# Fp4 feed-forward of a one-core Trainium2 program: normalisation and rounding exponent moved to ScalarE, rounding in three VectorE operations, scales double-buffered

## The reference, cut to what matters

```
xb = x.reshape(..., n // 16, 16)
scale = jnp.maximum(jnp.max(jnp.abs(xb), -1, keepdims=True) / 6.0, 1e-12)
xn = xb / scale
idx = jnp.searchsorted(_MID, jnp.abs(xn))       # grid 0, 0.5, 1, 1.5, 2, 3, 4, 6
q = _GRID[idx] * jnp.sign(xn) * scale
...
def fp4_linear(x, w):                           # gate, up and down
    return einsum('bsk,nk->bsn', fp4_quant_dequant(x), fp4_quant_dequant(w))
```

## Time and profile before

| what | value |
|---|---|
| device time, median of 3 runs | 3646.06 us (3645.56 to 3650.42) |
| the profiled execution: its time, as the span from first to last instruction | 3752.3 us |
| mean granted TensorE clock in it | 0.915 |
| busy over the span: PE / DVE / ACT / POOL | 84% / 67% / 53% / 32% |
| first pass of the stage: first operation to start of its last `add` | 18.82 to 182.15 us |
| second pass: the same | 899.2 to 1059.46 us |

### The profile page before, as it was taken

How to read it: one execution, slowest core, us unless ns; L and a number is a source line. 1 busy time by engine, 2 the same in 40 slices (tenths; PEclk the granted TensorE clock), 3 DMA queues, 4 the chain that set the end, 5 groups by cost and what they waited for, 6 DMA issues and landing times. The chain is left out here.

```text
span 3752.3 us, 61710 instructions
## 1 busy us (share of the span) xinstructions
PE 3149.9 (84%) x20415; PEld 1980.8 (53%) x20415; DVE 2516.1 (67%) x6929; ACT 1992.9 (53%) x2981; POOL 1210.8 (32%) x1282
## 2 busy tenths in 40 slices
PE   4669999786659967999999599687778885998899
PEld 2533333344448842222222488566666674887687
DVE  8888997675974468999995744543585345666565
ACT  1238988663214446999999144322332234664564
POOL 3454550112456631101010566366434651001000
PEclk8879999997859988999999699799898897999899
DMA  1043430000021132000000411401201113000100
GB/s 55 1 130 124 131 126 13 1 1 23 1 115 42 43 103 61 27 20 28 20 20 2 168 42 43 140 29 44 75 24 61 43 40 113 1 1 1 65 9 12
DMA packets 87167, 187.18 MB, mean 50 GB/s; under 512 B 23168, under 2 KB 41408, under 8 KB 83792
## 3 DMA queue, kind: packets, MB, share of 16 engines
q1 hardware_dynamic: 60048, 117.66, 9.3%
q0 software_dynamic: 26816, 65.58, 5.7%
HBM read 121.23 MB, written 61.34 MB: 49 GB/s over the span
## 5 line engine op out<-in xcount | busy, mean ns | idle before, releaser
L2486 ACT ACTIVATE core_pr<-core_two 128x1024 f32<-128x1024 f32 (+3 forms) x896 | 787.6, 935 | 49.3 <-PE core_two L2453 45.5
L2522 DVE TENSOR_REDUCE core_mx<-core_one 128x1 f32<-128x512 f32 x778 | 491.8, 685 | 20.9 <-PE core_one L2405 13.6
L2465 PE MATMUL core_ps_o<-core_pr,core_vals 128*32 128x512 f32 (+3 forms) x3584 | 434.5, 560 | 1.8 <-ACT core_oT L2497 1.5
L2405 PE MATMUL core_one<-arena,queries 64*128 64x512 bf16 (+3 forms) x1472 | 375.5, 363 | 29.8 <-PEq L62 19.6
L2453 PE MATMUL core_two<-queries,arena 64*128 64x512 bf16 (+3 forms) x1792 | 341.5, 360 | 9.4 <-ACT core_pr L2486 6.8
L2405 PEld LDWEIGHTS core_one<-arena,queries 64*128 64x128 bf16 x1472 | 113.3, 94 | 297.7 <-DVE core_mx L2522 132.4
L2339 POOL COPY core_vals<-arena 128x288 f32<-128x288 f32 x32 | 14.7, 459 | 692.1 <-PE core_ps_o L2465 692.1
L2516 DVE CUSTOM_DVE_ANT_0 core_junk<-core_one,core_over 128x512 bf16<-128x512 f32 (+4 forms) x334 | 201.9, 644 | 26.2 <-PE core_one L2405 21.4
L2453 PEld LDWEIGHTS core_two<-queries,arena 64*128 64x128 bf16 x1792 | 94.3, 94 | 201.7 <-ACT core_pr L2486 145.7
L2492 ACT ACTIVATE core_over<-core_two 128x1024 f32<-128x1024 f32 (+4 forms) x167 | 159.9, 958 | 58.4 <-PE core_two L2428 45.3
L424 POOL DMA_INDIRECT expert_out<-arena,moe_second_dest_index x142 | 139.9, 985 | 149.9 <-ACT arena L600 129.9
(11 more groups left out here) (614 smaller groups left out, 8184.0 us busy)
## 6 DMA issues: line engine op xcount, KB each, us to landing
arena<-expert_out SPq DMA_DIRECT2D x64, 256.0 KB, 3.8
expert_rows<-arena SPq DMA_DIRECT2D x13, 512.0 KB, 12.5
core_w_raw<-in_m_up POOLq DMA_DIRECT2D x25, 256.0 KB, 3.4
m_hi<-core_w_hi POOLq DMA_DIRECT2D x25, 256.0 KB, 2.4
m_lo<-core_w_lo POOLq DMA_DIRECT2D x25, 256.0 KB, 3.0
q_parts<-qkv_parts SPq DMA_DIRECT2D x16, 384.0 KB, 2.6
k_parts<-qkv_parts SPq DMA_DIRECT2D x16, 384.0 KB, 3.4
queries<-q_parts SPq DMA_DIRECT2D x64, 96.0 KB
```

The costliest lines, as they stand in the source:

```text
L2405: pe.matmul(one[bank[e]][:, 0:width], q_sb[rows, hq, pair, qt * P:(qt + 1) * P], k_sb[rows, hq, pair, kc * CW:kc * CW + width], start=True ...
L2465: mm = pe.matmul(ps_o[h * 32:(h + 1) * 32, off:CW], vals[:, hq % 2, j, h, :], pr[:, (n * N2 + k) % KEPT, h // 2, h % 2, off:CW], start=(j ...
L2486: a.activation(pr[:, step % KEPT, i, :, off:CW], two[spot[e] % 2][:, :, off:CW], ACT.Exp, scale=HD ** -0.5).then_inc(s_wide, 1)
L2522: v.tensor_reduce(at, scores, AX.X, ALU.max).then_inc(s_read, 1)
```

## The change

In `ffn0_stage`:

- `normalise` moves from VectorE to ScalarE, as scale and shift of an activation. GpSimd's `power` gains two small operations for the shift (minus mean times reciprocal deviation) and a wait for `normalise` of two chunks before.
- The rounding exponent is made on ScalarE by a new method `grid`: the square of the divided value, then a linear map. `round` on VectorE waits for it and has three operations in place of four (exponent mask and half bit in one, add, subtract).
- `scale` and `inverse` have two buffers each, so that new scales wait for `back` of two chunks before, not of the last one.
- The orders are rewritten. VectorE: all four `hidden(c+1)` and `x_scales(c+4)` come before `add(c-1)`, `fh.round(c)` and `h_scales(c+1)`. GpSimd: `fh.divide(c)` first and `h_back(c)` last in a turn. TensorE: `finish(c-1)` in place of `finish(c)`, ahead of `turn(c+3)` and the `up` of chunk c+2. ScalarE: two `silu`, `normalise(c+4)`, the four copies of `finish(c-1)`, `fh.grid(c)`, `copy(c+3)`, two `silu`, `x_grid(c+4)`.

The diff, cut to its core:

```diff
--- before.py
+++ after.py
@@ -1396,6 +1396,11 @@
 FP4_MAGIC = 1.5 * 2.0 ** 22
 BELOW = 1.0 - 2.0 ** -24
 EXPONENT = 0x7F800000
+HALF_BIT = 0x00400000
+
+
+GRID_SLOPE = 2.0 ** 22 / 6.0
+GRID_START = 8.0 * 2.0 ** 22 / 6.0
 
 
 class Fp4:
@@ -1406,75 +1411,69 @@
 
 
 
-    VEC_OPS = 7
-
-    def __init__(self, st, g, name, blocks):
-        self.g, self.nb = g, blocks
+    SCALES, STEPS = 3, 3
+
+    def __init__(self, st, g, name, blocks, binade):
+        self.g, self.nb, self.binade = g, blocks, binade
         self.amax = st.sb(f"{name}_amax", [P, blocks])
-        self.scale = st.sb(f"{name}_scale", [P, blocks])
-        self.inverse = st.sb(f"{name}_inverse", [P, blocks])
+        self.scale = st.sb(f"{name}_scale", [P, 2, blocks])
+        self.inverse = st.sb(f"{name}_inverse", [P, 2, blocks])
         self.v = st.sb(f"{name}_v", [P, blocks * BLOCK])
         self.magic = st.sb(f"{name}_magic", [P, blocks * BLOCK])
 
...
+        self.s_scales, self.s_square, self.s_grid, self.s_steps, self.s_pool, self.s_out = (
+            st.sem(f"{name}_{n}") for n in ("scales", "square", "grid", "steps", "pool", "out"))
+
+    def cut(self, ap):
+        return ap.rearrange("p (b k) -> p b k", k=BLOCK)
+
+    def largest(self, v, src, r):
+        v.tensor_reduce(self.amax[:], src, AX.X, ALU.max, apply_absolute_value=True).then_inc(self.s_scales, 1)
+
+    def inverted(self, v, r):
+        at = r * self.SCALES
+        if r >= 2:
+            v.wait_ge(self.s_out, r - 1)
+        v.wait_ge(self.s_scales, at + 1)
+        v.tensor_scalar(self.scale[:, r % 2], self.amax[:], 1.0 / 6.0, 1e-12, ALU.mult, ALU.max).then_inc(self.s_scales, 1)
+        v.wait_ge(self.s_scales, at + 2)
+        v.reciprocal(self.inverse[:, r % 2], self.scale[:, r % 2]).then_inc(self.s_scales, 1)
+
+    def divide(self, p, src, r):
+        p.wait_ge(self.s_scales, (r + 1) * self.SCALES)
+        if r:
+            p.wait_ge(self.s_out, r)
+        p.tensor_tensor(self.cut(self.v[:]), src, self.inverse[:, r % 2].unsqueeze(2).to_broadcast([P, self.nb, BLOCK]),
+                        ALU.mult).then_inc(self.s_pool, 1)
+
+    def grid(self, a, r):
+
+        a.wait_ge(self.s_pool, r + 1)
+        a.activation(self.magic[:], self.v[:], ACT.Square).then_inc(self.s_square, 1)
+        a.wait_ge(self.s_square, r + 1)
+        a.activation(self.magic[:], self.magic[:], ACT.Identity, bias=self.binade[:], scale=GRID_SLOPE).then_inc(self.s_grid, 1)
+
+    def round(self, v, r):
+        x, b, at = self.v[:], self.magic[:], r * self.STEPS
+        v.wait_ge(self.s_grid, r + 1)
+        v.tensor_scalar(b.bitcast(U32), b.bitcast(U32), EXPONENT, HALF_BIT, ALU.bitwise_and, ALU.bitwise_or).then_inc(self.s_steps, 1)
+        v.wait_ge(self.s_steps, at + 1)
+        v.scalar_tensor_tensor(x, x, BELOW, b, ALU.mult, ALU.add).then_inc(self.s_steps, 1)
+        v.wait_ge(self.s_steps, at + 2)
+        v.tensor_tensor(x, x, b, ALU.subtract).then_inc(self.s_steps, 1)
+
+    def back(self, p, dst, r):
+        p.wait_ge(self.s_steps, (r + 1) * self.STEPS)
+        q, scale, nb = self.cut(self.v[:]), self.scale[:, r % 2], self.nb
+        wide = scale.unsqueeze(2).to_broadcast([P, nb, BLOCK])
...
     def wait_done(self, eng, r):
-        eng.wait_ge(self.s_out, r + 2)
+        eng.wait_ge(self.s_out, r + 1)
 
...
@@ -1582,8 +1581,10 @@
     st = Stage(nc, name, prefetch)
     f = Front(st, g)
     head = Head(st, g, ahead) if ahead else None
-    fx = Fp4(st, g, "zq", CW // BLOCK)
-    fh = Fp4(st, g, "hq", CT * FFN0 // BLOCK)
+    binade = st.sb("binade", [P, 1])
+    fx = Fp4(st, g, "zq", CW // BLOCK, binade)
+    fh = Fp4(st, g, "hq", CT * FFN0 // BLOCK, binade)
+    minus, shift = st.sb("minus", [P, 2, CT]), st.sb("shift", [P, 2, CT])
     xq = st.sb("xq", [P, 2, CT, P])
     s = st.sb("silu", [P, 2, FFN0])
     h = st.sb("h", [P, 2, CT, FFN0])
...
@@ -1608,37 +1609,21 @@
     with st.block() as block:
         @block.vector
         def _(v):
-            fx.on(v)
-            fh.on(v)
             v.sem_inc(s_h, 2)
             v.sem_inc(s_sum, 1)
-            v.memset(hq[:], 0.0).then_inc(s_zero, 1)
+            v.memset(binade[:], GRID_START).then_inc(s_binade, 1)
 
             def statistics(c):
                 if c <= last:
+                    if c >= 2:
+                        v.wait_ge(s_shift, c - 1)
                     f.statistics(v, c, c % 2)
 
-            def normalise(c):
-                if c > last:
-                    return
-                if c == 0 and f.head:
-                    v.sem_inc(f.s_xn, 1)
-                    return
-                v.wait_ge(f.s_rstd, c + 1)
-                if c >= 2:
-                    v.wait_ge(fx.s_pool, c - 1)
-                for k in range(CT):
-                    end = v.tensor_scalar(f.xn[:, c % 2, k, :], flat(tile_of(g.x, c * CT + k)), f.mv[:, c % 2, k, 0:1],
-                                          f.rstd[:, c % 2, k:k + 1], ALU.subtract, ALU.mult)
-                end.then_inc(f.s_xn, 1)
-
             def x_scales(c):
-                if c > last:
-                    return
-                v.wait_ge(f.s_xn, c + 1)
-                fx.largest(v, blocks(f.tiles(c)), c)
-                fx.scaled(v, c)
-                fx.inverted(v)
+                if c <= last:
+                    v.wait_ge(f.s_xn, c + 1)
+                    fx.largest(v, blocks(f.tiles(c)), c)
+                    fx.inverted(v, c)
 
             def x_round(c):
                 if c <= last:
@@ -1650,17 +1635,11 @@
                 v.wait_ge(s_silu, c * CT + t + 1)
                 v.tensor_tensor(h[:, c % 2, t, :], s[:, t % 2, :], ps_u[t % 2][:, 0:FFN0], ALU.mult).then_inc(s_h, 1)
 
...
+            def h_scales(c):
+                if c <= last:
+                    v.wait_ge(s_h, c * CT + CT + 2)
+                    fh.largest(v, blocks(h[:, c % 2]), c)
+                    fh.inverted(v, c)
 
             def add(c):
                 v.wait_ge(s_down, c + 1)
@@ -1669,40 +1648,34 @@
 
             statistics(0)
             statistics(1)
-            normalise(0)
             x_scales(0)
             statistics(2)
+            v.memset(hq[:], 0.0).then_inc(s_zero, 1)
             x_round(0)
-            normalise(1)
             x_scales(1)
+            statistics(3)
+            x_round(1)
             hidden(0, 0)
             hidden(0, 1)
-            statistics(3)
-            x_round(1)
-            normalise(2)
             x_scales(2)
             hidden(0, 2)
             hidden(0, 3)
-            h_largest(0)
+            h_scales(0)
             statistics(4)
             x_round(2)
-            normalise(3)
             x_scales(3)
-            h_inverses(0)
             for c in range(CHUNKS):
                 hidden(c + 1, 0)
                 hidden(c + 1, 1)
                 statistics(c + 5)
                 x_round(c + 3)
-                normalise(c + 4)
-                fh.round(v, c)
+                hidden(c + 1, 2)
+                hidden(c + 1, 3)
+                x_scales(c + 4)
                 if c:
                     add(c - 1)
-                hidden(c + 1, 2)
-                hidden(c + 1, 3)
-                h_largest(c + 1)
-                x_scales(c + 4)
-                h_inverses(c + 1)
+                fh.round(v, c)
+                h_scales(c + 1)
...
@@ -1712,8 +1685,22 @@
         @block.gpsimd
         def _(p):
             def power(c):
-                if c <= last:
-                    f.power(p, c, c % 2)
+                u = c % 2
+                if c > last:
+                    return
+                if c == 0 and f.head:
+                    p.sem_inc(f.s_ve, 1)
+                    p.sem_inc(s_minus, 1)
+                    p.sem_inc(f.s_rstd, 1)
+                    p.sem_inc(s_shift, 1)
+                    return
+                if c >= 2:
+                    p.wait_ge(f.s_xn, c - 1)
+                f.power(p, c, u)
+                p.tensor_scalar(minus[:, u, :], f.mv[:, u, :, 0], -1.0, None, ALU.mult).then_inc(s_minus, 1)
+                p.wait_ge(f.s_rstd, c + 1)
+                p.wait_ge(s_minus, c + 1)
+                p.tensor_tensor(shift[:, u, :], minus[:, u, :], f.rstd[:, u, :], ALU.mult).then_inc(s_shift, 1)
 
             def x_divide(c):
                 if c <= last:
@@ -1737,16 +1724,18 @@
             power(3)
             x_back(1)
             x_divide(2)
+            p.wait_ge(s_zero, 1)
+            fh.divide(p, blocks(h[:, 0]), 0)
             power(4)
             x_back(2)
             x_divide(3)
-            p.wait_ge(s_zero, 1)
             for c in range(CHUNKS):
-                fh.divide(p, blocks(h[:, c % 2]), c)
+                if c:
+                    fh.divide(p, blocks(h[:, c % 2]), c)
+                power(c + 5)
+                x_back(c + 3)
+                x_divide(c + 4)
                 h_back(c)
-                x_back(c + 3)
-                power(c + 5)
-                x_divide(c + 4)
...
@@ -1801,15 +1790,33 @@
```

(50 more changed lines are left out.)

60 lines of the change are left out of this document (4 added, 56 removed).

## The result

The changed kernel takes 3718.6 us (median of 4 runs, 3714.5 to 3729.3) where the kernel before takes 3647.8 beside it: ratio 1.0203, 95% interval 1.0187 to 1.0219, or 70.8 us more. I had predicted 3714 us (3676 to 3743), 90% for slower. The profiled execution took 3715.8 us.

The account below looks back on a forecast made before the run. A ring of waits across engines was to bound the kernel: three intervals of 21.57 us, three of 19.83 and one of 16.63 make 140.8 against 103.1; less 3 at the start, 69.4 us slower in both passes, 3714 us (3676 to 3743).

Parts of the forecast that it names:

- a ring: Waits from h rounding through scales, `hidden`, `up`, copies and grid to the next rounding: 21.57 us with `normalise`, 19.83 without.
- the hold: VectorE's small operation in h's scales is held until GpSimd's `h_back` ends, making the scales term 3.50 us instead of 2.62.
- the first rival: VectorE still bounds, with turns 2.77 us shorter while x lasts and 0.93 later: 3612 us, chance 7%.
- to TensorE: First `hidden` of chunk c+2 on VectorE, with a gap before it and the step to TensorE: 0.66 us.
- two `up`: Two `up` on TensorE behind its wait for `hidden`: 4.13 us, against 2.36 at full clock.
- to the first copy with `normalise`: From the two `up` to ScalarE's first copy: 2.3 us with `normalise` between, 0.56 without.
- copies: ScalarE's four copies of `finish` with TensorE's turns between them: 3.82 us.
- grid: ScalarE's square and map on h, 1.35 and 1.44 us, with gaps and the step to VectorE: 2.96 us.
- The last interval: Seventh interval between h roundings, with no `up` left: rounding, `h_back`, turns and copies at low clock, grid, 16.63 us.
- the rival of the low clock lasting into the copies: TensorE's turns and copies take 6.73 us instead of 4.38 in each of six intervals: 3742 us, chance 8%.
- The start: Before the first h rounding, VectorE loses work: gain between 0 and 8.8 us a pass, taken as 3.
- The table rival: Square and SiLU on ScalarE share no table, so the ring holds one more 1.28 us load: 3736 us, chance 6%.

Follow-up runs that it names:

- e1: Operations of the kernel before (`normalise` and four-step rounding on VectorE, single scales) in the changed kernel's order: 3726.7 us, ratio 1.0226.
- e9: Changed kernel with one VectorE list altered, the scales of h behind `hidden` instead of ahead: ratio 1.0069 to the kernel before.
- e3: Changed kernel with ScalarE's `normalise(c+4)` moved ahead of the two SiLU: 3711.9 us, ratio 1.0177 to the kernel before.
- e5: Changed kernel with the block maxima of h kept in PSUM: ratio 1.0166 to the kernel before.
- e6: Changed kernel with 45 unread transposes added on TensorE in its wait ahead of `up(c+2,0)`: ratio 1.0145 to the kernel before.
- e4: Changed kernel with `normalise(c+4)` and `fh.grid(c)` ahead of SiLU(c+1,2..3) on ScalarE, and VectorE rounding before it adds: 3656.1 us, ratio 1.0022.
- e2: The changed kernel's operations in the order of the kernel before, h's grid behind the SiLU of tiles 2 and 3: 3720.6 us, ratio 1.0202.
- e7: e2 with h's grid on ScalarE right behind the four copies of chunk c: ratio 1.0146 to the kernel before.
- e8: Kernel before, in its order, with `normalise` and x's exponent on ScalarE and scales double-buffered; h keeps four VectorE operations: ratio 1.0038.
- e11: e8 with the x rounding on VectorE behind the h rounding and the addition: ratio 1.0011 to the kernel before.
- e12: e8 with x's exponent ahead of ScalarE's copies, x's scales ahead of h's, GpSimd dividing x before h: 3622.5 us, ratio 0.9939 to the kernel before.

## Why the prediction was right, point by point

**That a ring decides, and which one.** The order alone brings the loss (e1), though there the ring closes through `add(c-1)`. Letting `hidden` pass the scales takes 3 to 7 us out of each of the first six intervals and two thirds of the loss out of the total (e9). Single links were shortened one by one: `normalise` in e3, the hold in e5, the clock in e6. That h's grid closes the ring in the changed kernel is read from its trace, where it comes last, and borne out by e4, which opened `add` too. That VectorE idles, 14.61 busy of 23 us, rules out the first rival.

**The terms**, in the interval from 83.63 to 106.70, predicted and measured: rounding 4.20, 4.21; scales with the hold 3.50, 3.53; to TensorE 0.66, 0.53; two `up` 4.13, 4.76; to the first copy with `normalise` 2.3, 2.10; copies 3.82, 5.13; grid 2.96, 2.81. Sum 21.57, and 23.07. Two terms were too small, both of the clock. Behind a wait of 7.28 us (before: 4.90) nearly all products of the two `up` run at half clock (1.2 of 2.4 GHz), where before the last ones were back at full clock; over the pass the two `up` take 3.99 to 4.83 us, 4.49 in the mean. And in the early turns TensorE stands 2.12 us before 99.27 while ScalarE normalises. The three transposes at 96.66 had run at full clock (0.49 us) and so did the next three at 99.27 (0.55), but those from 100.61 on took 0.85. In the late turns nothing stands there: the copies go from 162.32 to 166.14 us, 3.82 as predicted, and the intervals are 19.5 to 20.2 (predicted 19.83). e3 shows that it is `normalise` that does it: moved, the early copies take 3.83 too. The last interval was 16.54 (16.63). This is near the rival of the low clock lasting into the copies, at about half of its price and in three intervals of seven, but by another way: the low clock did not last, it came back. The pass came to 144.4 us instead of 140.8.

**The start.** The first h rounding came at 61.32 instead of 64.02 us: 2.7 earlier, where I took 3.

**The hold.** L1438 took 1.16 us, as the text said; e5 shows it by changing only where the source lies.

**ScalarE's operations.** Groups of the first pass, from 40 us on:

```profile
L1454 ACT ACTIVATE ffn_first_hq_magic<-ffn_first_hq_magic,ffn_first_binade 128x1408 f32<-128x1408 f32 x8 | 11.8, 1469 | 0.3
L1452 ACT ACTIVATE ffn_first_hq_magic<-ffn_first_hq_v 128x1408 f32<-128x1408 f32 x8 | 11.0, 1378 | 0.0
...
L1817 ACT ACTIVATE ffn_first_ln_xn<-x,ffn_first_shift,ffn_first_ln_rstd 128x128 f32<-128x128 f32 x16 | 6.5, 481 | 0.0
```

1.38 and 1.47 us stand where 1.35 and 1.44 were worked out from shorter operations. The Trainium skill ("ScalarE: Activation LUTs", section "What ACT_TABLE_LOAD costs") would by its formula give 1.36 and 1.45 as an estimate; both are within 2%. The table rival fell: behind the kernel's start the first pass has this one load ahead of its first SiLU, as the kernel before has (at 31.81 us), the second has one too (944.38), and no Square brings another.

```profile
33.21 1.28 ACT L1826 ACT_TABLE_LOAD   x1
```

**From stage to total.** 37.7 + 3.6 of the ring, less 2.7 at the start, make 38.6 us in the first pass, whose last addition starts 38.5 later (220.62 instead of 182.15). Twice that is 77; at the end of both passes 72.5 us are left and in the total 70.8. Why some 4.5 us are missing at the end of the second pass no run shows. I had 69.4 against the span; the error of 3.6 us a pass and this difference nearly cancel, so that the total fits better than its parts is luck.

**What the reasoning lacked.** That the order closes a ring was right; that it was the only one was not, and e2, e7, e8 and e11 each met another. The prediction spoke of one ring; the turn is the longest of several, all near 20 us: e2's through SiLU(c+1,3), e8's through the x exponent, e1's through `add(c-1)`, and the changed kernel's own. That through `add` was in the changed kernel as well, 1.1 us behind the grid, so a faster grid alone could have given at most that in a turn. What is not settled is how low the changed kernel could go with h's exponent on ScalarE: e4's 1.0022 was the best of that kind tried, and e12's lists were not tried with it.
